# A packed rest of the patch convolution and reordered stretches in a fused vision-tower kernel

## What is computed

```python
pe = conv(x, conv_w, stride 14)            # 81 patches, K = 3*14*14 = 588, N = 256
red = mean of the 9 patches of a window
kv = LN(win) @ la_wkv ; q = LN(red) @ la_wq ; local_out = red + softmax(q k) v @ la_proj + b
h = concat(local_out @ mod_w + mod_b, class token with global attention)      # (128, 10, 256)
h = h + attention(LN(h))                   # layer 0: 16 heads of 16, 10 tokens, two scores masked
h = h + moe(LN(h))                         # 8 experts, top 2, 256 -> 1024 gelu -> 256, LN of each
h = h + causal attention(LN(h))            # layer 1: scores clipped to +-10
x = LN(h)                                  # low rank, layer 1
h = h + x @ base_W + b + (x @ sA) @ sB + sum over the top 2 of 6: w_e * (x @ A_e) @ B_e
```

## Time and profile before

| | us |
|---|---|
| median of 3 runs | 823.07 (822.62 to 823.4) |
| profiled execution, its own time | 819.8 |
| its span | 817.7 |
| mean granted clock of PE | 0.941 of full |

### The profile page before, as it was taken

One profiled execution on the slowest core, in us unless ns is written; L12 is line 12 of the kernel. 1 busy time (PEld: TensorE's weight loads), 2 busy tenths in 40 slices (PEclk: granted clock), 3 DMA queues, 4 the chain that ended last, 5 costly groups with the idle time before them and its releaser, 6 DMA issues.

```text
span 817.7 us, 12959 instructions
## 1 busy us (share of the span) xinstructions
PE 716.3 (88%) x4311; PEld 616.5 (75%) x4311; DVE 508.0 (62%) x1233; ACT 374.7 (46%) x935; POOL 414.1 (51%) x279
## 2 busy tenths in 40 slices
PE   3979999999999999999808755999999999495978
PEld 3869998988989898655607645999999999353866
DVE  3668787778778677769799561222222222588956
ACT  3555565656556555533131422444444444165251
POOL 3755757677575761348849602433333432226820
PEclk9989999999999999999967956999999999699899
DMA  8642223212312120000020065889988881400001
GB/s 260 189 131 66 69 90 89 73 62 89 90 56 79 45 79 25 1 1 0 1 104 1 37 264 215 322 321 309 341 332 336 328 308 71 166 6 1 1 1 64
DMA packets 34487, 102.73 MB, mean 126 GB/s; under 512 B 3624, under 2 KB 12152, under 8 KB 27000
## 3 DMA queue, kind: packets, MB, share of 16 engines
q1 hardware_dynamic: 31832, 94.84, 33.5%
q0 software_dynamic: 2592, 7.10, 2.3%
HBM read 95.75 MB, written 6.17 MB: 125 GB/s over the span
## 4 chain that ended last, share of the span: by engine, by line
PE 73%; POOL 9%; DVE 9%; issue 2%; DMA 2%; ACT 2%; POOLq 1%; SPq 0%; DVEq 0%; ACTq 0%
PE banks L1631 12%; PE banks L1639 11%; PE banks L287 10%; PE banks L289 10%; PE banks L288 10%; PE banks L294 6%; PE banks L300 4%; POOL a_prod L1155 3%; PE banks L1285 2%; POOL a_prod L1170 2%; PE banks L1315 2%; POOLq L282 1%; PE banks L1969 1%; DVE banks L1438 1%; POOL rstd L336 1%
## 5 line engine op out<-in xcount | busy, mean ns | idle before, releaser
L401 POOL TENSOR_TENSOR x_lo<-xraw,x_hi 128x640 fp32r<-128x640 f32 x81 | 128.5, 1594 | 105.1 <-ACT x_hi L395 105.1
L287 PE MATMUL banks<-wc_hi,x_hi 128*128 128x256 f32 x405 | 120.6, 298 | 14.2 <-POOL x_lo L401 14.1
L1729 ACT ACTIVATE hid<-banks,b 128x128 f32<-128x128 f32 x216 | 79.3, 367 | 109.9 <-PE banks L1631 109.9
L288 PE MATMUL banks<-wc_lo,x_hi 128*128 128x256 f32 x405 | 115.7, 286 | 0.0
L289 PE MATMUL banks<-wc_hi,x_lo 128*128 128x256 f32 x405 | 115.6, 286 | 0.0
L287 PEld LDWEIGHTS banks<-wc_hi,x_hi 128*128 128x128 f32 x405 | 78.4, 194 | 16.3 <-issue 14.8
L1888 DVE TENSOR_TENSOR res<-banks,xb 128x256 f32<-128x256 f32 x27 | 11.5, 424 | 127.1 <-PE banks L1639 127.1
L288 PEld LDWEIGHTS banks<-wc_lo,x_hi 128*128 128x128 f32 x405 | 78.5, 194 | 1.8 <-issue 0.2
L424 DVE BATCH_NORM_STATS2 stats<-banks 128x6 f32<-128x256 f32 x81 | 34.7, 428 | 71.8 <-ACT pe_sb L418 71.1
L418 ACT ACTIVATE pe_sb<-banks 128x256 f32<-128x256 f32 x81 | 31.0, 383 | 105.4 <-PE banks L289 105.4
L289 PEld LDWEIGHTS banks<-wc_hi,x_lo 128*128 128x128 f32 x405 | 78.4, 194 | 0.0
(11 more groups left out here) (306 smaller groups left out, 1707.2 us busy)
## 6 DMA issues: line engine op xcount, KB each, us to landing
w_raw<-in_w SPq DMA_DIRECT2D x28, 1024.0 KB, 6.7
xraw<-in_x_main SPq DMA_DIRECT2D x27, 768.0 KB
w1more<-in_w SPq DMA_DIRECT2D x13, 1024.0 KB, 5.6
w2more<-in_w SPq DMA_DIRECT2D x13, 1024.0 KB, 8.2
xraw<-in_x_rest SPq DMA_DIRECT2D x27, 114.0 KB
yl<-y_rows SPq DMA_DIRECT2D x2, 1028.0 KB, 7.0
a_w<-in_qkv_w SPq DMA_DIRECT2D x2, 768.0 KB, 5.4
x_rows<-w_raw SPq DMA_DIRECT2D x5, 256.0 KB, 2.0
```

What stands on the lines that cost most here:

```text
L287: pe.matmul(dst, a[0], b[0], start=start, stop=False)
L288: pe.matmul(dst, a[0], b[1], start=False, stop=False)
L401: pool.tensor_tensor(x_lo[:, i % RING_X, :], xraw[:, k].rearrange("p c b -> p (c b)"), x_hi[:, i % RING_X, :], ALU.subtract).then_inc(sem( ...
L1729: act.activation(hid[:, s % 2, fc, :], bank(fc % 2, 0, P), ACT.Gelu, bias=b1[:, bass.ds(e * FC + fc, 1)]).then_inc(sem("gelu_made"), 1)
```

## The change

**Rest of the convolution.** The rest of 76 rows is loaded several times: rows 0 to 63 twice into chunk 4 (partitions 0 and 64), all 76 into chunk 5, and rows 64 to 75 twice more into chunk 5 (partitions 76 and 96). The weights' chunks hold w_hi and w_lo accordingly, and POOL subtracts in place in x_hi for chunk 5's first 76 partitions. So chunk 4 is x_hi times (w_hi | w_lo), chunk 5 has x_lo w_hi and the two products of the last 12 rows: 4 x 3 + 2 = 14 matmuls. x_hi is 768 wide instead of 640, x_lo is 512, POOL has two instructions for a patch, load_x issues six DMAs instead of two, the weights' rest four more.

**Prologue.** ACT rounds four patches ahead of its copies (BEHIND) instead of two; the steps between move to later places; POOL's roots stand behind patches 9 and 13 instead of 6 and 12.

**Attention 0.** POOL makes the score products of three tiles instead of two before the root of the class token. The maxima and sums lie in PSUM and DVE's steps of the two halves are interleaved otherwise. POOL's last value tile (t = 8) comes in two parts without a fold, and PE sums nine or ten keys instead of half of them. project_o(7) and the first group's logits, with norms and copies on ACT, stand before turn_o(8) on PE, and the top two of that group after add_o(7) on DVE.

**Attention 1.** Row 7's channel sum goes from DVE to PE (bank 6), the first softmax half comes a step earlier, the last value tile is in two parts too, and tiles 0 to 3 of the low-rank part (`pe_lora(pe, 0)`, `act_lora(act, 0)`) stand before turn_o(8).

**Low rank.** No barrier. The base weights are joined to z_w: one product with 374 columns in one bank (5), turned tiles in one bank (4), ACT copies the 374 columns, POOL adds the base part to h, the bias is an extra row of z_b. Routing runs in two parts, tiles 0 to 7 and 8, 9; ACT's exp and copies of both come after all of its tiles. The five adds go into h and come after both parts on DVE. The low-rank tiles' memory lies in w_raw.

```diff
-KC = 5
+KF = 4
+KC = KF + 2
+KREST = 588 - KF * P
+REST = ((KF, 0, 0, HALF_A), (KF, HALF_A, 0, HALF_A), (KF + 1, 0, 0, KREST), (KF + 1, KREST, HALF_A, OVER),
+        (KF + 1, LOW_W, HALF_A, OVER))
...
+            for c, at, first, rows_here in REST:
+                sp.dma_start(xraw[at:at + rows_here, a:b, c, :], ...)
...
+            rest = x_hi[0:KREST, i % RING_X, (KC - 1) * P:KC * P]
+            pool.tensor_tensor(rest, xraw[0:KREST, k, KC - 1], rest, ALU.subtract).then_inc(sem("x_lo_made"), 1)
...
-            pe.wait_ge(sem("x_lo_made"), i + 1)
-            for c in range(KC):
+            pe.wait_ge(sem("x_lo_made"), 2 * i + 2)
+            for c in range(KF):
                 a = [x[:, k, c * P:(c + 1) * P] for x in (x_hi, x_lo)]
-                last = mm3(pe, bank(i % 2), a, (wc_hi[:, c, :], wc_lo[:, c, :]), c == 0, c == KC - 1)
+                mm3(pe, bank(i % 2), a, (wc_hi[:, c, :], wc_lo[:, c, :]), c == 0, False)
+            for c in range(KF, KC):
+                last = pe.matmul(bank(i % 2), x_hi[:, k, c * P:(c + 1) * P], wc_hi[:, c, :], start=False, stop=(c == KC - 1))
...
-            pool_scores(pool, 0, 4, 6)
+            pool_scores(pool, 0, 4, 7)
             inverse_std(pool, *batch_of("attention 0", 3))
-            pool_scores(pool, 0, 6, T)
+            pool_scores(pool, 0, 7, T)
...
+        ROW_ON_PE = T - 3
...
+        def add_channels(pe, dst, slot, n):
+            by_channel = slot[:, 0:n * C].rearrange("p (x d) -> p x d", d=D16)
             for ch in range(D16):
-                last = pe.matmul(bank(b, 0, n * H16), ident[:, :], by_channel[:, :, ch], start=(ch == 0), stop=(ch == D16 - 1))
+                last = pe.matmul(dst, ident[:, :], by_channel[:, :, ch], start=(ch == 0), stop=(ch == D16 - 1))
...
             for t in range(T):
                 turn_o(t)
-                if t:
+                if t and t != T - 2:
                     project_o(t - 1)
+                if t == T - 3:
+                    project_o(t)
+                    if layer == 0:
+                        pe_logits(pe, 0)
+                    else:
+                        pe_lora(pe, 0)
...
-                    if t == T - 1:
+                    if t == T - 2:
                         softmax_half(dve, link, 1, 0)
...
+        def pe_lora(pe, g):
+            a, b = GROUPS[g]
...
+            turn_z(a)
+            for t in range(a, b):
                 pe.wait_ge(sem("z_xT_made"), t + 1)
+                if t + 1 < b:
+                    turn_z(t + 1)
+                if t:
+                    pe.wait_ge(sem("z_made"), t)
+                mm_rows(pe, bank(5, 0, ZW + C), z_xT[:, t % 2, :], z_w, 0, ZW + C).then_inc(sem("z_done"), 1)
...
+        def act_lora(act, g):
...
+            def copy_z(t):
+                act.wait_ge(sem("z_done"), t + 1)
+                act.activation(z[:, t, :], bank(5, 0, ZW + C), ACT.Copy).then_inc(sem("z_made"), 1)
...
+        ROUTED = [(0, 8), (8, T)]
+
+        def act_lora_out(act):
+            for i in range(2):
+                a, b = ROUTED[i]
+                act.wait_ge(sem("z_l_made"), i + 1)
+                act.activation(z_p[:, a:b, :], z_l[:, a:b, :], ACT.Exp).then_inc(sem("z_exp_made"), 1)
+                for t in range(a, b):
...
+        def dve_lora_out(dve):
             for t in range(0, T, 2):
+                dve.wait_ge(sem("z_h_made"), t + 2)
                 dve.wait_ge(sem("z_out_done"), t + 2)
+                dve.tensor_tensor(h_at(t, 2), out_bank(t, 2), h_at(t, 2), ALU.add).then_inc(sem("z_out_made"), 1)
...
-            phase(pe, 3)
-            pe_lora(pe)
+            pe_lora(pe, 1)
+            pe_lora(pe, 2)
+            pe_lora_out(pe)
...
+                if BEHIND <= i < LEAD - 1 + BEHIND:
+                    copy_pe(act, i - BEHIND)
```

More of the change, by code:

```diff
@@ L1116, in used_count @@
             done = pool_jobs(0) * layer + pool_jobs(layer)[:i + 1]
[L1117 removed]
+            here = done[len(pool_jobs(0)) * layer:]
+            return len(done) - sum(summed_on_pe(layer, t, kind) for t, kind, _ in here) - layer * len(SUMS_ON_PE)
         def score_products(eng, kind, t, n, slot):
```

461 lines of the change are left out of this document (244 added, 217 removed).

## The result

The changed kernel took 843.31 us (median of 4 runs, 841.95 to 847.7) beside 822.85 us of the kernel before on the same chip: ratio 1.0262, 95% interval 1.0233 to 1.0292. That is 20.5 us slower, where 821.6 us and a range of 813 to 830 had been forecast. The span of the profiled execution went from 817.7 to 842.3 us.

The account below looks back on a forecast made before the run. It took PE to bound the steady tokenizer rounds, with waits elsewhere and one dependent chain in the low-rank tail. Terms -4.2 - 8.4 - 2.9 + 1.0 + 13.0 = -1.5 from 823.07 gave 821.6 us, range 813 to 830.

Parts of the forecast that it names:

- Rounds, -8.4: Tokenizer's steady rounds: one matmul less for each of 70 patches, 0.12 us each, saves 8.4 us; bounds -9 and -7.
- Prologue, -4.2: Before the first kv product: it comes at 42.4 in place of 46.64 us, 4.2 us earlier; bounds -6 and -2.
- 14 x 1.7 us of POOL from 12.8: Prologue: POOL's 14 low parts at 1.7 us each from 12.8, plus a root of 1.19, end at 37.8 us.
- Loads: Rival, prologue: 3.2 us for the DMA issues and POOL's 1.81 a patch make it no faster; 826 us, chance 0.12.
- Scores of attention 0, -2.9: Scores of attention 0: DVE's wait of 2.93 us for POOL's product goes, saving 2.9 us; bounds -3.3 and -1.
- Attention 0, end, +1.0: End of attention 0: early logits and a longer tile 8 sum delay the last h; costs 1.0 us, bounds -1.5 and +4.
- Attention 1, +6.6 to the last h: Attention 1: low-rank tiles 0 to 3 ahead of tile 8's sum put the last h at 793.5 instead of 786.86 us.
- a gain of 2.4 from row 7: Attention 1: row 7's reduction moves from DVE to idle PE, so DVE's last value tile ends 2.4 us earlier.
- Tail hidden: Rival, attention 1 and low rank: the early tiles hide and cost nothing; 813.5 us, chance 0.2.
- Low rank, +6.4: From the last h of attention 1 to the end: the low-rank stage becomes 6.4 us longer.
- Clock: Rival, low-rank tiles: PE's gaps lower its clock to 1.2 GHz, some +8 us; 830 us, chance 0.13.
- The gain is not realized: Rival, tokenizer rounds: the hand-over x_hi, x_lo, product bounds them, price +8.4 us; 830 us, chance 0.07.

Follow-up runs that it names:

- a_rest_only: The kernel before with the packed rest of the convolution and nothing else of the change; 824.01 us, ratio 1.0022 to the kernel before.
- best_packed: The kernel before with packed rest, ACT's new prologue order, 1.25 MB of weights loaded later and two POOL pauses; 817.38 us, ratio 0.9952.
- t_fold: The changed kernel with value tile 8 summed from folded halves as in the kernel before; 841.24 us, ratio 1.0249 to the kernel before.
- t_logits_late: The changed kernel with group 0's logits, copies and top two moved behind project_o(9) in attention 0; 837.87 us, ratio 1.0191 to the kernel before.
- t_lora_last: The changed kernel with low-rank tiles 0 to 3 moved behind the last h of attention 1; 841.7 us, ratio 1.0244 to the kernel before.

## Why the prediction was wrong

**Rounds, -8.4: right**, -7.0 in this trace, -8.2 in a_rest_only's, -8.1 in best_packed's. PE at 34.00 of 34.00 us, POOL's two instructions at 1.27 and 0.46 us.

**Prologue, -4.2: wrong sign, +8.1.** The step that failed is the cost of the loads, at most "3.2 (eight issues of 0.40 each)" and taken as +1.5, and with it "14 x 1.7 us of POOL from 12.8", which took POOL for the limit. The bound was made for the first group alone and with too low a price: SP was through with that group's rest 4.6 us later, and the first rounding came 3.6 us later. The groups behind it had no term: patch 9's rest was issued 12.3 us later, ACT waited 5.14, 1.57 and 1.78 us for x, and POOL, which was to run 14 low parts on end, stood 7.93 us for ACT ahead of patch 9's. The trace of the kernel before had the warning in its DMA share, 0.91 from 10 to 20 us. The rival "Loads" named the right place, but by the first issues and POOL's 1.81, not by what followed; it led to 826 with a chance of 0.12. DVE's stall behind POOL was half seen ("1.49 each while POOL runs a low part"): beside several low parts on end it was 4.53. How much of the +8.1 this stall adds to the loads stays open.

**Scores of attention 0, -2.9: mechanism right, size -0.8.** DVE's wait of 2.93 us is gone, but in this execution it waited 2.4 us in all for PE ahead of the class token's work, 0.7 before, with a granted clock of 0.89 instead of 1.00 in the 15 us around the longer of these waits. In t_fold and t_logits_late, with the same code there, the stage gained 2.7 and 2.4.

**Attention 0, end, +1.0: +5.8.** The forecast's start of the sum, about 464, was near (465.42). Its length was not: 7.48 us for 40 records in place of 4.7, and half clock stood only in the upper bound, which +5.8 exceeds all the same. And "the last group ends about where it did" failed: its copy came at 483.79 instead of 477.69. The last h was 9.2 us late instead of 4.9, and the six tiles of logits behind it took 7.1 us where ten had taken 10.2: they gave back 3.1 us, and 4.9 had been counted on. By t_logits_late the failed step is the price of the early logits on PE, +4.3, not the longer sum.

**Attention 1, +6.6 to the last h: +11.1.** The sum counted on a gain of 2.4 from row 7. DVE's last value tile ended 7.1 us later than before in a stage that began 6.6 later, so no gain was left. The sum of row 7 on PE was not given a price: it took 7.14 us at full clock, 223 ns a record, and DVE waited 0.86 us for it. At its next reduction DVE was still 1.4 us ahead (761.59 for 756.37, in a stage 6.6 later). It lost that in two waits of 0.80 and 0.93 us for copies of h, which came late because PE's first projection waited 2.23 us for ACT and then ran at a granted clock of 0.50. In t_lora_last and t_fold, with the same code up to there, 1.4 and 0.7 us of the gain remained, so 2.4 was too much and its size differs between executions. Cadence 2.1 instead of 1.9 us adds 0.6. The statement that a term in front of tile 8 lies on the path was right, and the rival "Tail hidden", with a chance of 0.2, is refuted: PE did not wait at tile 8's sum, and without the early tiles the last h came 12.8 us earlier (t_lora_last).

**Low rank, +6.4: +6.9.** Each step is there: exp 15.9 us after the last h (14.8 forecast), z_s at 21.1 (19.8), DVE's five adds last. Half clock for the outputs was priced at 1.6; the eight took 6.4 us from 826.03 against 8 x 0.59 = 4.7, so 1.7.

**Rivals.** "Clock" predicted a granted clock under 0.8 in both groups of tiles. In the tiles the products took 1.42 to 1.53 us and the granted clock was 1.00 (788 to 797 and 805 to 820 us); it fell in attention 0's sum, at the first projections of attention 1 and at the outputs instead. "The gain is not realized" was refuted by 34.00 of 34.00. The sum's two largest errors, 12.3 in the prologue and 9.3 in the attentions, have the same sign; a sum of -1.5 from terms of 4 to 13 us needed a wider range.

## What to carry to other kernels

Before trading matmuls for loads, look at the DMA share of the first microseconds and at the issuing queue: here 8 us saved in the rounds were lost ahead of them, until the first window's rest went in one piece again. Leave the first loads few and small. Work put ahead of a ready step on an in-order engine is a cost, not filling, unless a row shows the engine idle there for that long; and where it leaves short gaps, the step behind it can be slower too, as attention 0's sum was. When several parts are changed at once, build each alone: here the mended prologue, the packed rest and two small pieces gave 1.5% together, and the tail as a whole cost 2.6%.
